# A two-layer hybrid network on one core: the expert products of the streamed batches, begun eleven units later

## What is computed

```
attn = attention(q, k, v) @ Wo + bo                     # 16 heads of 8
x = layer_norm(src + attn, ln1_g, ln1_b)
keys = (x @ router_w + router_b)[..., 0]
expert_idx = remainder(floor(keys), 4)
for e in range(4):
    h = relu(x @ W1[e] + b1[e])                         # 128 -> 512
    y = h @ W2[e] + b2[e]                               # 512 -> 128
    ff_out = ff_out + where(expert_idx == e, y, 0.0)
return layer_norm(x + ff_out, ln2_g, ln2_b)
```

## Time and profile before

| | us |
|---|---|
| median of 3 runs | 4833.11 |
| lowest, highest | 4823.82, 4839.20 |
| profiled execution, own time | 4847.35 |
| its span | 4845.5 |
| PE busy | 3972.9 (82%) |
| DVE busy | 3183.2 (66%) |
| ACT busy | 2805.1 (58%) |
| POOL busy | 1147.4 (24%) |
| mean granted clock of PE | 0.878 |

### The profile page before, as it was taken

One profiled execution on the slowest core, in us unless ns is written; L12 is line 12 of the kernel. 1 busy time (PEld: TensorE's weight loads), 2 busy tenths in 40 slices (PEclk: granted clock), 3 DMA queues, 4 the chain that ended last, 5 costly groups with the idle time before them and its releaser, 6 DMA issues.

```text
span 4845.5 us, 92928 instructions
## 1 busy us (share of the span) xinstructions
PE 3972.9 (82%) x37240; PEld 1659.8 (34%) x37240; DVE 3183.2 (66%) x4646; ACT 2805.1 (58%) x5448; POOL 1147.4 (24%) x1376
## 2 busy tenths in 40 slices
PE   4888867877788768873998989888999999898982
PEld 2334344343344435551223232323222222233232
DVE  4777524444443367744987868677789999787832
ACT  2677622323212245430877778677889888777771
POOL 3221011010100103332222616162212122242413
PEclk7999988798886877865999999999999999999996
DMA  2222001001100000002113222222111111314112
GB/s 79 59 59 55 14 16 23 22 2 22 23 1 1 0 8 1 1 1 63 42 32 96 64 77 65 71 70 60 41 22 48 48 35 29 91 42 110 50 52 92
DMA packets 141118, 204.34 MB, mean 42 GB/s; under 512 B 51906, under 2 KB 88770, under 8 KB 140436
## 3 DMA queue, kind: packets, MB, share of 16 engines
q1 hardware_dynamic: 123924, 137.97, 11.5%
q0 software_dynamic: 16768, 60.49, 4.3%
HBM read 123.34 MB, written 64.68 MB: 39 GB/s over the span
## 4 chain that ended last, share of the span: by engine, by line
PE 54%; DVE 21%; ACT 7%; issue 6%; POOL 6%; DMA 4%; SPq 2%; POOLq 0%; DVEq 0%; ACTq 0%
PE ps L1117 11%; DVE stream_max_pieces L1317 8%; PE ps L1090 7%; PE ps L1102 5%; PE ps L545 3%; PE ps L1887 3%; PE ps L1203 2%; PE ps L504 2%; PE ps L1211 2%; PE ps L2578 1%; PE ps L255 1%; PE ps L1964 1%; PE ps L1963 1%; PE ps L1956 1%; ACT stream_probs L1229 1%
## 5 line engine op out<-in xcount | busy, mean ns | idle before, releaser
L1317 DVE TENSOR_REDUCE stream_max_pieces<-ps 128x2 f32<-128x1024 f32 x1536 | 1795.5, 1216 | 384.2 <-PE ps L1102 376.7
L1229 ACT ACTIVATE stream_probs<-ps 128x512 f32<-128x512 f32 x3072 | 1654.4, 600 | 335.5 <-PE ps L1090 313.3
L1117 PE MATMUL ps<-stream_probs,stream_v 128*16 128x256 f32 x12288 | 989.7, 395 | 31.7 <-issue 30.3
L1102 PE MATMUL ps<-stream_k_stack,stream_q_stack 48*128 48x512 bf16 x3072 | 661.9, 396 | 107.5 <-DVE stream_max_pieces L1317 75.2
L1090 PE MATMUL ps<-stream_q_stack,stream_k_stack 51*128 51x512 bf16 x3072 | 680.7, 396 | 24.5 <-ACT stream_probs L1229 8.2
L684 DVE TENSOR_REDUCE alibi_max_pieces<-ps 128x2 f32<-128x1024 f32 (+3 forms) x384 | 355.4, 952 | 140.2 <-PE ps L529 130.8
L625 ACT ACTIVATE alibi_probs<-ps 128x512 f32<-128x512 f32 (+3 forms) x768 | 333.8, 492 | 175.6 <-PE ps L510 142.0
L1117 PEld LDWEIGHTS ps<-stream_probs,stream_v 128*16 128x16 f32 x12288 | 203.8, 94 | 672.5 <-issue 390.0
L1090 PEld LDWEIGHTS ps<-stream_q_stack,stream_k_stack 51*128 51x128 bf16 x3072 | 181.9, 93 | 675.4 <-ACT stream_probs L1229 501.4
L309 POOL CAST stream_negmax_parts<-stream_negmax_t 128x32 bf16<-128x32 f32 x96 | 20.4, 212 | 1084.5 <-DVE stream_negmax_t L1306 1071.9
L1835 PE MATMUL ps<-delta_w_delta,ident 128*128 128x512 f32 x400 | 217.5, 676 | 63.0 <-DVE delta_branch_means L2209 28.3
(11 more groups left out here) (443 smaller groups left out, 5596.6 us busy)
## 6 DMA issues: line engine op xcount, KB each, us to landing
stream_q_terms_dram<-stream_q_parts SPq DMA_DIRECT2D x72, 256.0 KB
stream_k_terms_dram<-stream_k_parts SPq DMA_DIRECT2D x72, 256.0 KB
stream_q_stack<-stream_q_terms_dram SPq DMA_DIRECT2D x96, 192.0 KB
stream_k_stack<-stream_k_terms_dram SPq DMA_DIRECT2D x96, 192.0 KB
delta_v_shifted<-delta_v_padded SPq DMA_DIRECT2D x64, 158.0 KB, 3.5
alibi_q_terms_dram<-alibi_q_parts SPq DMA_DIRECT2D x24, 256.0 KB
alibi_k_terms_dram<-alibi_k_parts SPq DMA_DIRECT2D x24, 256.0 KB
alibi_q_stack<-alibi_q_terms_dram SPq DMA_DIRECT2D x32, 192.0 KB
```

The source lines that it names most:

```text
L1102: ins = e.matmul(c.ps[:, mbank(key) + r, :], qs[R, buf, pair, qt * P:(qt + 1) * P], ks[R, buf, pair, kh * 512:kh * 512 + 512], start=True, ...
L1117: ins = e.matmul(c.ps[32 * j:32 * j + 16, 7, Q], v[:, b % 2, kt, GH * g + j, :], pr[:, (u + j // 2) % RP, j % 2, Q], start=(n == 0 and k = ...
L1229: e.activation(pr[:, u % RP, r, :], c.ps[:, ebank(key), :], ACT.Exp, scale=SCALE).then_inc(s_ed, 1)
L1317: e.tensor_reduce(mx[:, j % 2, kh, 4 * pair + qt % 4, :], c.ps[:, mbank(key):mbank(key) + 2, :], AXX, ALU.max).then_inc(s_md, 1)
```

## The change

Only positions in `Stream.behind` move. `slots` goes from 70 to 74; the transposes from 73, 74, 75 to 84, 85, 86; the eleven `h` from 77, 81, ..., 117 to 88, 92, ..., 128; the six `w2` from 86, 94, 102, 110, 118, 119 to 97, 105, 113, 121, 129, 131; the five late weight gathers from 88, 88, 96, 96, 104 to 98, 98, 106, 106, 114; `ystore` from 121 to 132, `gather` from 126 to 138, `stats, 1` from 145 to 156 and `scale, 1` from 146 to 157. `scatter` at 53 and the six first weight gathers (37 to 67) stay. No instruction is added, removed or altered.

```
-            yield (37, 40, 43, 46, 63, 67)[j] if j < NWB else 88 + 8 * ((j - NWB) // 2), ("weights", n, j)
-        yield 70, ("slots", n)
+            yield (37, 40, 43, 46, 63, 67)[j] if j < NWB else 98 + 8 * ((j - NWB) // 2), ("weights", n, j)
+        yield 74, ("slots", n)
...
-        yield 121, ("ystore", n)
-        yield 126, ("gather", n)
+        yield 132, ("ystore", n)
+        yield 138, ("gather", n)
```

10 lines of the change are left out of this document (5 added, 5 removed).

## The result

The changed kernel took 4787.14 us, median of ten executions (4765.02 to 4800.45); the kernel before took 4830.81 us in the ten beside it on the same chip. The ratio is 0.9905, with a 95% interval from 0.9884 to 0.9926: 43.7 us or 0.9% faster. The forecast was 4772 us. The time lies inside the range and the sign is right, but only about 44 of the 61.5 us came.

A forecast was written before the change was run, and what follows sets the result against it. PE paces the stream but stands for the sorted tokens in six batches. Terms -71.1 + 14.6 - 10 + 0 + 0 + 5 = -61.5 us, off the median 4833.11, gave 4772 us; range 4752 to 4808.

The forecast's parts named there:

- six waits go: PE's waits for `slots` at the first transpose in batches 1 to 4, 9 and 10 vanish: -71.1 us.
- waits that are left: `slots` behind the maxima of position 73: about 1.0 us in five batches, 5.1 and 4.3 in batches 3, 4; +14.6 us.
- POOL inside the batches: Moved gather and `scale` steps on POOL delay nobody, with 13.9 us of cover before DVE's L1395: 0 us.
- tail: After the last unit, later `ystore` and gather delay POOL's inverse root, all paid: +5 us, bounds 3 and 8.
- The clock: At the transposes, PE's granted clock stays up without the long waits: -10 us, bounds 0 and 13.
- The products, put at 0: Moved `h` and `w2` cost PE the same, even across the batch border: 0 us, bounds -10 and +25.
- My own test for being wrong: Wrong if units 64 to 84 miss 1.18 us each, or first 32 positions of batches 2-5, 10 grow over 4 us.
- The sign that I gave for it: In the profile, from the last unit to the end takes 4 to 5 us longer, POOL's L1543 directly before L1491.
- The maxima hold the slots: Rival, chance 0.18: maxima write-to-read takes 8.0 us, seven waits 3.6 us longer each, clock falls in all; 4804 us.
- The border is paid: Rival, chance 0.12: products moved to positions 0 to 4 push DVE's norm, output and statistics six times; 4797 us.
- POOL's queue: Rival, chance 0.03: gather waits on POOL for `ystore`, delaying `scale, 0` and DVE's key; slower than before, 4853 us.
- The remaining two: Rivals: all `slots` waits go (0.08, 4756 us); `slots` moves with the transposes, waits stay (0.02, 4833 us, up to 5 more).

The follow-up runs named there:

- e5: The kernel before, unchanged, traced on the third chip: 4899.14 us (one execution).
- e6: The changed kernel, unchanged, run on the third chip: 4880.87 us, ratio 0.9965 to the kernel before.
- e1: The changed kernel with the `slots` load back at position 70 instead of 74, second chip: 4885.17 us (one execution), ratio 0.997.
- e2: The changed kernel with `scale, 1` at 166 instead of 157, second chip: 4872.13 us (one execution), ratio 0.994.
- e7: The changed kernel with `stats, 1` and `scale, 1` back at 145 and 146, third chip: 4867.17 us, ratio 0.9929.
- e4: The kernel before with transposes at 84 to 86 and `h`, `w2` packed closer so none crosses the border, second chip: 4878.13 us, ratio 0.9950.
- e3: The kernel before with only `stats, 1` and `scale, 1` moved to 156 and 157, second chip: 4886.03 us (one execution), ratio 0.997.

## Why the prediction was right, and where it wasn't

Step by step, in us, for the pair of traces on the first chip:

| term of the sum | forecast | measured |
|---|---|---|
| six waits go | -71.1 | -71.1 |
| waits that are left | +14.6 | +25.5 |
| clock, and products over the border | -10 + 0 | -14.6 |
| POOL inside the batches | 0 | +17.0 |
| tail | +5 | +6.1 |
| sum | -61.5 | -37.1 |

The measured terms come from the stretches: the waits by their rows; the third term is the change of units 64 to 127 beyond the waits (-28.9), that of units 0 to 31 of all batches (+11.1) and that of the step from the last unit to the output transposes (+3.2); the fourth is units 32 to 47 of all batches. Their sum meets the 37.2 us of the traces. The medians say 43.7, with an interval from 36 to 56.

The time came out within 15 us of the forecast, but part of that is luck. In the traces the waits left cost 11 us more than forecast and POOL 17 us more, and the clock gave 9 to 10 us less; some 14 us of gain from the products, which the forecast had at 0, made up for a part.

*The bound was read rightly.* The chain, the list of waits and the timeline named one wait at six places, and most of the gain hangs on it: e5 shows the same code on a chip where this wait is nearly absent, and there the change brings 16 us.

*The waits left: the mechanism held, its term was mis-sized.* SP's order is the one given. From the traces, the chain behind the begin of unit 73 (us; the last line is when PE is at its transposes):

| step | forecast | b1 | b2 | b3 | b4 | b9 | b10 | b11 |
|---|---|---|---|---|---|---|---|---|
| to the write of the maxima | 3.5 (7.6, 6.8 in b3, b4) | 3.5 | 5.1 | 7.7 | 7.0 | 3.5 | 4.3 | 3.5 |
| write to read | 4.4 | 5.7 | 5.5 | 5.4 | 5.8 | 4.5 | 6.5 | 4.2 |
| read to `slots` | 1.3 | 1.3 | 1.3 | 1.3 | 1.3 | 1.3 | 1.3 | 1.3 |
| `slots` to the transposes | 4.8 | 4.8 | 4.8 | 4.9 | 4.8 | 4.8 | 4.8 | 4.8 |
| PE is there after | 13.0 | 12.8 | 12.8 | 12.8 | 12.8 | 12.8 | 12.8 | 12.8 |

The step from write to read was taken from batch 11 (4.4 us), where no stack load is in flight, and it is 5.4 to 6.5 us in five of the six batches that have one. Batches 2 and 10 also begin the write late, behind the load. In e6, where PE is late and the load left SP some 7 us or more before the write, the same step takes 3.6 to 4.6 us. I had an upper bound of 8.0 for it and took the value nearest to the least loaded row. The row for the landing held. The Trainium skill's price (DMA: Bandwidth & Descriptors, section "Anatomy of one DMA"), by which the prediction worked out 3.7 us, is given there for DMAs that GpSimd issues, while SP issues `slots`; measured are 4.8 us.

*The clock: this step failed.* I took 10 of the 13 us, on the premise that the short waits would be 1 us and would leave the clock up. Of those four, three were 2.5 to 4.1 us, and behind the fourth, 1.32 us in batch 9, the clock fell too. From the first transpose of batch 9 to its third unit the changed kernel takes 4154.18 - 4148.39 = 5.79 us, hardly less than the 6.05 of before. Compared with e1's 25.0 us for units 80 to 95, the six batches lose 1.5 to 2.9 us each beyond the wait itself, 12 us together, about as much as before. So the clock gave nothing or 1 us. The length of the wait alone doesn't decide it. In batch 10 of e2 the clock fell behind 0.98 us, in batch 10 of e7 it stayed up behind 1.95 us. The transposes of e2, and a window behind them (columns as above):

```profile
4432.79 0.65 PE L1195 MATMUL ps<-ident,stream_slots 128*128 128x128 f32 x4 [0.98 <-DMA stream_slots<-stream_slots_dram]
```

```profile
4434.00:4437.00 3.00, 3.00 (x20) 1.01 (x24) 1.23 (x2) 2.04 (x5) 0.00 (x0) 0.50 0.00 0
```

The same two views of e7:

```profile
4437.98 0.66 PE L1195 MATMUL ps<-ident,stream_slots 128*128 128x128 f32 x4 [1.95 <-DMA stream_slots<-stream_slots_dram]
```

```profile
4439.00:4442.00 3.00, 3.00 (x32) 1.46 (x31) 2.28 (x2) 2.82 (x6) 0.00 (x0) 1.00 0.00 0
```

What else decides it isn't shown here.

*The products, put at 0.* If the clock gave 0 to 1 us, the rest of the third term, some -14 us, belongs to the products at their new places. That is beyond my bound of -10, on the good side. Why they cost less there isn't shown. That they are hidden where DVE holds PE up, behind the border, is one reading; against it speaks e4, which gains 17 us in units 64 to 127 with packed products and none behind the border.

*POOL inside the batches: this step failed, and it is the largest miss.* I asked whether anyone would wait for POOL's results, found 13.9 us of cover, and wrote 0. That was true: L1395 waits for nothing of POOL. I didn't ask what POOL's work would run beside. Before, `scale, 1` ended at 2744.56 in batch 2 and the small steps of the key chain began at 2744.61; eleven units later it runs beside them, and both work on SBUF. e2, e3 and e7 show it from three sides: 17 us. My own test for being wrong, the first 32 positions longer by more than 4 us, looked sixteen units too early.

*The tail: +6.1 us, for the reason given.* About 1 us of the miss is the landing of `ystore`, 5.06 us instead of 4.1. The sign that I gave for it, "from the last unit to the end 4 to 5 us longer", didn't come: that stretch grew from 135.7 to 144.9 us, 9.3 us, since 3.2 us of products now stand between the last unit and the output transposes. I had left these out of the sign, though they are the same products that I had moved over the border.

*The rivals.* "The maxima hold the slots" came half: the step is 5.4 to 5.7 us and not 8.0, the waits are 11 us longer than forecast and not 25, and the clock fell in six of seven. "The border is paid" fell: units 0 to 31 grew by 11 us in all, less than the 29 us by which the second halves shrank beyond the waits. "POOL's queue" fell inside the batches and is the tail's 6.1 us, where the forecast had it. The remaining two didn't happen on the first chip.

*What stays open.* Why PE, ACT and DVE stand on the second and third chip while eight indirect transfers run. The transfers are there in every case, the moved gather takes its standing along, and in batches 6 to 8, which have none, there is no standing; but no run spaced them on such a chip. Open too are what decides whether the clock falls behind a short wait, and what made the products cheaper.

## What to carry to other kernels

When a step moves on an engine that isn't the bottleneck, ask two questions: who waits for its result, and whose memory traffic it now runs beside; a step with ample cover can still hold up a neighbour. A request that is put behind a write and its read-back on one queue inherits their latency under the load that is in flight there, so take that latency from a row with the same transfers ahead of it: here the cleanest row said 4.4 us and the busiest 8.0, and it was 4.2 to 6.5. And a gain that consists of one wait is worth what that wait is on the chip at hand: here 44 us on one, 16 on another.

## What the runs showed of the hardware

- The granted clock fell from 1.0 to 0.50 behind waits of PE of 0.98 us (e2, batch 10) and 1.32 us (the changed kernel, batch 9, where it stayed down for over 3 us). It stayed at 1.0 behind waits of 0.99 us (the changed kernel, batch 11) and 1.95 us (e7, batch 10).
- DVE steps on 128x8 elements in SBUF took 2.35 and 2.20 us instead of 0.2 beside a 128x1024 product of POOL. DVE's reductions out of PSUM (L1317), and the one-input reduction L1395 out of SBUF, weren't touched.
- The write and read-back of the maxima through DRAM took 3.6 to 4.6 us with no stack load just ahead of it (e6) and 5.4 to 6.5 us behind one in five batches of the changed kernel (4.5 us in batch 9).
- The same kernel had medians of 4826 to 4831 us on the first, fourth and fifth chip and of 4897 to 4899 us on the second and third. In the two traces of it the difference up to the output transposes is 68 us: 25 us more standing of PE (103 us at L1090, in 42 waits of up to 6.1 us, less the waits for the slots that it hides), and 44 us more busy time at a mean granted clock of 0.93 instead of 0.95.
